# Graph kernel in five sweeps over one adjacency matrix: neighbour masks counted ahead, in the first sweep

## What is computed

```python
# layer 0
Ax = adj @ h;  x += 1 - 0.1*h - 0.01*sum(h*Ax, axis=1)
# layer 1, two hops
for k in range(2): h = tanh(concat([adj @ h, h], axis=1) @ W[k])
# layer 2: only the last 100 neighbours of a row, halved for each later one
support = h @ weight
mask = (adj != 0); rank = cumsum(mask, axis=1); deg = rank[:, -1:]
k = minimum(deg, 100); pos = rank - (deg - k)
w = mask * where(pos > 0, 0.5 ** (k - pos), 0)
x += w @ support + bias
# layer 3
h1 = tanh(concat([h, t], axis=1) @ W1 + b1)
x += h1 @ W2 + b2 + adj @ (h @ B.T) - sum(adj, axis=1) * (h @ B.T)
```

## Time and profile before

| | us |
|---|---|
| median of 3 runs | 831.64 (830.78 to 833.84) |
| the profiled execution | 832.51 |
| its span, first to last instruction | 830.7 |
| PE busy | 739.1 (89%) |
| DVE busy | 445.3 (54%) |
| ACT busy | 200.5 (24%) |
| POOL busy | 126.3 (15%) |
| DMA, over the whole span | 275.16 MB, 331 GB/s |

### The profile page before, as it was taken

How to read it: one execution, slowest core, us unless ns; L and a number is a source line. 1 busy time by engine, 2 the same in 40 slices (tenths; PEclk the granted TensorE clock), 3 DMA queues, 4 the chain that set the end, 5 groups by cost and what they waited for, 6 DMA issues and landing times.

```text
span 830.7 us, 10008 instructions
## 1 busy us (share of the span) xinstructions
PE 739.1 (89%) x3717; PEld 293.7 (35%) x3736; DVE 445.3 (54%) x765; ACT 200.5 (24%) x287; POOL 126.3 (15%) x148
## 2 busy tenths in 40 slices
PE   3877878889999999999999798889888979999998
PEld 1222222223433344444444243334333433343333
DVE  5111111147666676767667788888888852111110
ACT  2000000000100000100001576566656640211111
POOL 5001111110000001221112201101110113322221
PEclk9999999999999999999999899999999999999999
DMA  9999999999999999999899666667666747999995
GB/s 375 416 420 419 421 420 421 419 375 376 398 389 389 388 385 346 342 359 334 336 361 362 223 226 221 241 222 266 216 246 221 266 165 277 349 348 368 374 360 208
DMA packets 45984, 275.16 MB, mean 331 GB/s; under 512 B 5104, under 2 KB 13424, under 8 KB 13552
## 3 DMA queue, kind: packets, MB, share of 16 engines
q1 hardware_dynamic: 36720, 266.13, 83.0%
q10 hardware_dynamic: 9216, 8.39, 3.0%
HBM read 270.31 MB, written 4.19 MB: 330 GB/s over the span
## 4 chain that ended last, share of the span: by engine, by line
PE 44%; DMA 27%; DVE 22%; issue 4%; POOL 2%; ACT 1%; DVEq 1%; POOLq 0%
PE accA L922 31%; DMA land<-adj_blocks 26%; DVE uS L757 16%; PE tr L822 2%; PE spare L934 2%; PE spare L937 2%; PE nat L846 1%; PE nat L842 1%; PE accA L947 1%; POOL rstd L434 1%; PE spare L877 1%; DVE uS L740 1%; DVE st L626 1%; PE nat L838 1%; DMA xin<-x_rows 1%
## 5 line engine op out<-in xcount | busy, mean ns | idle before, releaser
L922 PE MATMUL accA<-land,X 128*64 128x512 f32 x1504 | 352.5, 598 | 23.1 <-DMA land<-adj_blocks 21.9
L922 PEld LDWEIGHTS accA<-land,X 128*64 128x64 f32 x1504 | 100.7, 136 | 214.4 <-issue 144.5
L582 ACT ACTIVATE wS<-spare 128x1024 uint16<-128x1024 f32 x128 | 131.0, 1024 | 86.7 <-PE spare L937 84.1
L922 PE MATMUL accA<-cache,X 128*64 128x512 f32 x544 | 131.9, 605 | 22.1 <-DVE X L787 12.6
L757 DVE SCALAR_TENSOR_TENSOR uS<-land,uS 128x512 bf16<-128x512 f32 x180 | 128.5, 714 | 19.7 <-DVE uS L757 0.5
L934 PE MATMUL spare<-uS,triA 128*128 128x512 bf16 x248 | 94.7, 386 | 31.2 <-DVE uS L757 28.4
L441 POOL TENSOR_TENSOR hS<-tS 128x256 f32<-128x256 f32 x32 | 25.7, 805 | 561.8 <-DVE tS L627 561.8
L937 PE MATMUL spare<-uS,triB 128*128 128x512 bf16 x246 | 94.3, 383 | 0.5 <-ACT wS L582 0.2
L740 DVE TENSOR_TENSOR wS<-wS,land 128x512 f32<-128x512 f32 x96 | 66.8, 695 | 39.4 <-DMA land<-adj_blocks 36.8
L740 DVE TENSOR_TENSOR uS<-uS,land 128x512 f32<-128x512 f32 x92 | 64.6, 702 | 32.4 <-DMA land<-adj_blocks 29.6
L947 PE MATMUL accA<-wS,X 128*128 128x512 bf16 x247 | 74.5, 381 | 0.3
(11 more groups left out here) (76 smaller groups left out, 436.2 us busy)
## 6 DMA issues: line engine op xcount, KB each, us to landing
land<-adj_blocks SPq DMA_DIRECT2D x235, 1024.0 KB, 7.6
cache<-adj_blocks SPq DMA_DIRECT2D x17, 1024.0 KB, 12.8
xin<-x_rows ACTq DMA_DIRECT2D x32, 128.0 KB, 6.2
x_rows<-zS ACTq DMA_DIRECT2D x24, 128.0 KB, 4.7
cache<-x_rows SPq DMA_DIRECT2D x1, 1024.0 KB, 4.9
out_rows<-zS ACTq DMA_DIRECT2D x8, 128.0 KB, 7.0
wts<-weights SPq DMA_DIRECT2D x1, 675.0 KB, 6.2
cache<-triangles SPq DMA_DIRECT2D x1, 128.0 KB, 6.0
```

The costliest lines, as they stand in the source:

```text
L582: nc.scalar.activation(weights(c, b).bitcast(U16), spare[:, 2 * k:2 * k + 2, :].rearrange("p a b -> p (a b)"), ACT.Relu)\
L922: last = nc.tensor.matmul(accA[k * D:(k + 1) * D, c % 2, :], tile(X[p % 2], TQ * b + k), of[:, k * W:(k + 1) * W], start=(b == 0), stop=(b ...
```

## The change

- L0 now also makes the masks: DVE writes the mask of a whole block (two tiles, 1024 elements, bfloat16) in one instruction, and PE multiplies it with a 0/1/128 matrix (`count`), one block behind the sweep, into `spare`. For each tile this gives, per row of the matrix, the count of non-zero entries in all later tiles. After each chunk ACT copies one half of the result, DVE adds the other, and an ACT DMA writes it to DRAM (`counts_d`).
- L2 passes the matrix forward. DVE makes plain masks, one instruction for a block, of 127 partitions; the 128th partition is filled by small DMAs from the counts (`counts_for`, one for each pair, on SP's queue). So one triangular matrix for a tile does, with the count of later tiles as one of its terms: the second matmul of each tile goes.
- Partition 127 of each tile is then missing from the weights. It is done apart for each chunk: SP loads these 32 rows (`left_over`, nine small DMAs), POOL makes their weights in three instructions, and PE adds them in one matmul. The features of that partition take a way through DRAM once (`left_d`, `loS`).
- Two of the 16 evictions of weights of a chunk (blocks 4 and 12) go from ACT to DVE, three blocks late in DVE's list.
- Row sums: 10 blocks in L1A, 6 in L1B (before 8 and 8).
- 16 pairs are cached, 48 are loaded in each later sweep. The eight mask places are of a whole block. A place in `land` is free in L0 only after the masks too.

```diff
 def cached_pairs(c):
-    return (0, 1, 4) if c == 0 else (0, 4)
+    return (0, 4)
...
+TOTALS = {L1A: (1, 2, 4, 5, 7, 9, 10, 12, 13, 15), L1B: (0, 3, 6, 8, 11, 14)}
...
+MASKS = 8
+AHEAD = 3
+EVAC_DVE = (4, 12)
+EVAC_LAG = 3
...
+        def weights_out(eng, ops, c, b):
+            n = NQ * c + b
+            eng.wait_ge(tri_done, n + 1)
+            if n >= WRING:
+                eng.wait_ge(w_used, n - WRING + 1)
+            k = b % 2
+            w, of = weights(n).bitcast(U16), spare[:, 2 * k:2 * k + 2, :].rearrange("p a b -> p (a b)")
+            if b in EVAC_DVE:
+                ops.tensor_scalar(w, of, 0.0, None, ALU.max).then_inc(w_ready_dve, 1)
+            else:
+                ops.activation(w, of, ACT.Relu).then_inc(w_ready, 1)
...
+            def counts_for(g):
+                if g < MASKS // 2:
+                    sp.wait_ge(sums_done, 2 * g + 2)
+                else:
+                    sp.wait_ge(tri_done, 2 * (g - MASKS // 2) + 2)
...
+                sp.dma_start(uS[LAST:P, at:at + 2 * BLK].rearrange("o (t w) -> o t w", w=W),
+                             tile_counts[c, 4 * k:4 * k + 4, 0].rearrange("(o t) w -> o t w", o=1))\
+                    .then_inc(counts_in[g % (MASKS // 2)], 16)
+            def left_over(c):
+                if c:
+                    sp.wait_ge(left_ready, c)
+                rows = adj_in.rearrange("(b p) (t w) -> p b t w", p=P, t=2 * TQ)
+                for k in range(PAIRS):
+                    sp.dma_start(loadjS[4 * k:4 * k + 4, :], rows[LAST, c * PAIRS + k]).then_inc(left_in, 16)
+                sp.dma_start(locntS[:, :], tile_counts[c, :, 1]).then_inc(left_in, 16)
+            def after_masks(g):
+                for i in range(counts_to[0], min(g + AHEAD, PAIRS * NC - 1) + 1):
+                    counts_for(i)
+                    counts_to[0] = i + 1
+                if g % PAIRS == 3 and g // PAIRS + 1 < NC:
+                    left_over(g // PAIRS + 1)
+                if g == 6:
+                    sp.wait_ge(copy_used, copied_no(L1B, NC - 1, 1) + 1)
+                    sp.dma_start(left_d, X[1][LAST:P, :].bitcast(F16)).then_inc(left_rows, 16)
+                    sp.wait_ge(left_rows, 16)
+                    sp.dma_start(loS[:, :], left_d.rearrange("o (t w) -> (o t) w", w=2 * D)).then_inc(left_rows, 16)
...
             def step(p, c, before, before2):
-                for k in pair_order(p):
+                if p == L2 and c == 0:
+                    sp.wait_ge(counts_out, 16 * NC)
+                    left_over(0)
+                    after_masks(0)
+                for k in range(PAIRS):
...
-                        if pp == L2:
-                            sp.wait_ge(u_ready, NT * pc + 2 * (NQ - 1 - 2 * pk) + 2)
-                        else:
+                        if pp != L2:
                             sp.wait_ge(swept, sweep_no(pp, pc, 2 * pk + 1) + 1)
+                        if pp in (L0, L2):
+                            sp.wait_ge(u_ready, mask_no(pp, pc, 2 * pk + 1) + 1)
...
+                    if n >= LAND and pp == L2:
+                        after_masks(PAIRS * pc + pk)
...
+            def left_over(c):
+                w = left_weights(c)
+                pool.wait_ge(left_in, 16 * (PAIRS + 1) * (c + 1))
...
+                nc.gpsimd.tensor_scalar(loadjS[:, :], loadjS[:, :], 0.0, -NEIGH * BIT, ALU.is_equal, ALU.mult)\
+                    .then_inc(left_step, 1)
...
+                nc.gpsimd.tensor_tensor(loadjS[:, :], loadjS[:, :], locntS[:, :], ALU.subtract).then_inc(left_step, 1)
...
+                nc.gpsimd.tensor_scalar(w, loadjS[:, :], NEIGH * BIT, 0.0, ALU.add, ALU.max).then_inc(left_ready, 1)
...
+                if p == L0 and at == 4:
+                    act.wait_ge(counted, NQ * (c + 1))
+                    if c:
+                        act.wait_ge(count_ready, c)
+                    nc.scalar.activation(upperS, spare[D:P, c % 2, :], ACT.Copy).then_inc(count_half, 1)
+                if p == L0 and at == 7:
+                    act.wait_ge(count_ready, c + 1)
+                    act.dma_start(counts_d[c], countS).then_inc(counts_out, 16)
...
                     if at == 7:
                         norm_rows(p, c, chunk(X[1], c))
+                        dve.wait_ge(count_half, c + 1)
+                        if c:
+                            dve.wait_ge(counts_out, 16 * c)
+                        nc.vector.tensor_tensor(countS, upperS, spare[0:D, c % 2, :], ALU.add).then_inc(count_ready, 1)
...
-                            nc.vector.scalar_tensor_tensor(out=u, in0=of, scalar=0.0, in1=earlier,
-                                                           op0=ALU.not_equal, op1=ALU.add).then_inc(u_ready, 1)
+                if p in (L0, L2):
+                    n = NQ * c + b
+                    wait_landed(dve, p, c, b)
+                    if n >= MASKS:
+                        dve.wait_ge(counted if p == L0 else tri_done, n - MASKS + 1)
+                    elif p == L2:
+                        dve.wait_ge(sums_done, b + 1)
+                    rows = P if p == L0 else LAST
+                    nc.vector.tensor_scalar(masks(b)[0:rows, :], block_of(p, c, b)[0:rows, :], 0.0, None, ALU.not_equal)\
+                        .then_inc(u_ready, 1)
+                if p == L2 and b - EVAC_LAG in EVAC_DVE:
+                    weights_out(dve, nc.vector, c, b - EVAC_LAG)
...
+            def count(c, b):
+                pe.wait_ge(u_ready, mask_no(L0, c, b) + 1)
+                if b == 0 and c >= 2:
+                    pe.wait_ge(count_ready, c - 1)
+                for k in range(TQ):
+                    t = TQ * b + k
+                    last = nc.tensor.matmul(spare[k * D:(k + 1) * D, c % 2, :], later[:, 2 * (NT - t):2 * (2 * NT - t)],
+                                            masks(b)[:, k * W:(k + 1) * W], start=(b == 0), stop=(b == NQ - 1))
+                last.then_inc(counted, 1)
...
+            def triangle(c, b):
+                n, g = NQ * c + b, PAIRS * c + b // 2
+                pe.wait_ge(u_ready, mask_no(L2, c, b) + 1)
+                pe.wait_ge(counts_in[g % (MASKS // 2)], 16 * (g // (MASKS // 2) + 1))
+                if n >= 2:
+                    weights_ready(n - 2)
+                for k in range(TQ):
+                    last = nc.tensor.matmul(spare[:, 2 * (b % 2) + k, :], triA[:, :], masks(b)[:, k * W:(k + 1) * W],
+                                            start=True, stop=True)
                 last.then_inc(tri_done, 1)
...
+                if b == NQ - 1:
+                    pe.wait_ge(left_ready, c + 1)
+                    if c == 0:
+                        pe.wait_ge(left_rows, 32)
+                    nc.tensor.matmul(accA[:, c % 2, :], loS[:, :], left_weights(c).bitcast(BF16),
+                                     start=False, stop=True).then_inc(weighed, 1)
```

More of the change, by code:

```diff
@@ L60, in cached_before @@
     return sum(len(cached_pairs(k)) > i for k in range(c))
[L63 to L70, removed]
 LAND = 4
-LOADS = [(p, c, k) for p in range(5) for c in range(NC) for k in pair_order(p) if (c, 2 * k) not in CACHE_SLOT]
+LOADS = [(p, c, k) for p in range(5) for c in range(NC) for k in range(PAIRS) if (c, 2 * k) not in CACHE_SLOT]
 LOAD_NO = {what: i for i, what in enumerate(LOADS)}
@@ L136, in norm_no, with mask_no, evac_no @@
     return PRO_GROUPS + row_no(p, c)
-HELD = 2
+MASKS = 8
+AHEAD = 3
 WRING = 4
[L145 to L166, removed]
+EVAC_DVE = (4, 12)
+EVAC_LAG = 3
+LAST = P - 1
+def mask_no(p, c, b):
+    return (0 if p == L0 else NQ * NC) + NQ * c + b
+def evac_no(c, b):
+    on_dve = sum(k in EVAC_DVE for k in range(NQ))
+    if b in EVAC_DVE:
+        return on_dve * c + EVAC_DVE.index(b)
+    return (NQ - on_dve) * c + sum(k not in EVAC_DVE for k in range(b))
 LATE = (8,)
@@ L476, in step @@
                         split_rows(before[1])
+                if p == L2 and c + 1 < NC:
+                    left_over(c + 1)
                 if p == L3 and c:
@@ L941, in weigh @@
-            def weigh(c, pair):
-                pe.wait_ge(w_ready, NQ * c + pair + 1)
-                first = 2 * weigh_order(c)[0]
-                for i in range(2):
-                    t = 2 * pair + i
-                    w = weights(c, pair)[:, i * W:(i + 1) * W].bitcast(BF16)
-                    last = nc.tensor.matmul(accA[:, c % 2, :], tile16(NT - 1 - t), w,
-                                            start=(t == first), stop=(t == NT - 1))
-                last.then_inc(w_used, 1)
+                if p == L0 and b:
+                    count(c, b - 1)
+                elif p == L0 and c:
+                    count(c - 1, NQ - 1)
@@ new lines, in weigh @@
+            def weigh(c, b):
+                n = NQ * c + b
+                weights_ready(n)
+                if c == 0 and b % 2 == 0:
+                    pe.wait_ge(copy_used, copied_no(L1B, b // 2, 1) + 1)
+                for k in range(TQ):
```

(15 more changed lines are left out.)

121 lines of the change are left out of this document (55 added, 66 removed).

## The result

The changed kernel takes 795.55 us (median of 4 runs, 788.66 to 798.05) against 831.21 for the kernel before: ratio 0.9553, 95% interval 0.9485 to 0.962. The forecast was 773, in a range of 755 to 798: faster, as said, but by 36 us where 58 were forecast. The execution whose profile is shown took 788.66 us, the fastest of the four, its span is 786.6. Runs of this kernel lie 9 us apart, those of the kernel before 3.5; part of that shows in the clock of L2, as experiment 1 tells.

A forecast was written before the change was run, and what follows sets the result against it. The prediction took loads (DMA) to bound L0, PE to bound L1A and L1B, DVE to bound L2. Its terms, +4 + 1 - 4.5 - 15 - 45 = -59.5 us, from 832.5 gave 773, range 755 to 798.

The forecast's parts named there:

- Masks, evictions, counts beside the sweep: Prices: 0.67 us a mask in L0, 1.23 a DVE eviction in L2; L0's counts, 3.4 a chunk on PE, hidden.
- L0's start, "4 us later": In L0, the fifth load waits for masks until 23.2, DMA idles from 21.2 to 25.6, L0 ends 4 us later.
- L1A, "+1": L1A: ten blocks of row sums stay below PE; L0's last count and layer norm add 1 us (0 to 3).
- L1B, "-4.5": L1B: fewer row sums on DVE remove most of PE's gaps, layer norm waits included: 4.5 us less (0 to 6).
- L2's start, "15 less": L2's first two chunks end at t0 + 49 after the sweep's end t0, before t0 + 63.6: 15 us less (11 to 20).
- The stall that was forecast instead: L2, chunk 1: PE's list stands still 6 us at block 1 for `loS`, landing at t0 + 32.5 but needed at t0 + 26.
- L2 steady, "20.0": L2's later chunks: DVE's list takes 20.0 us a chunk; six chunks at 20.0 in place of 27.6, 45 less.
- POOL's lock: In steady L2, masks stand still while POOL works in SBUF: 2.8 us a chunk (0 to 4.9).
- POOL holds up DVE in full: Rival, L2: all 4.9 us of POOL count and layer norms come late, 3.5 a chunk more, 794 us; chance 0.17.
- L0 becomes PE's: Rival, L0: counts don't run side by side, PE needs 21.8 a chunk against 20.6, 10 us more, 783; chance 0.08.

The follow-up runs named there:

- experiment 1: The changed kernel run again, unaltered, against the kernel before: 792.17 us (median of the three executions that count), ratio 0.9504.
- Experiment 2: Changed kernel with PE taking up the counts in chunk 0 of L0 only from block 6 on: 794.65 us, 0.9542 of the kernel before.
- experiment 4: Changed kernel with row sums of eight blocks each in L1A and L1B again: 794.8 us, 0.9546 of the kernel before.
- experiment 11: Changed kernel with late first L0 counts, L2's first loads before the row-sum wait, and early x rows in L2: 780.79 us, 0.9378 of the kernel before.
- experiment 10: Changed kernel with x rows loaded early in L2 and no count transfers there behind the first four pairs: 787.67 us, 0.9461 of the kernel before.
- Experiment 3: Changed kernel with L2's loads of pairs 1, 2, 3 and 5 issued before SP's wait for row sums: 786.75 us, 0.944 of the kernel before.
- experiment 6: Changed kernel with POOL's three instructions for left-over rows on 8 columns in place of 512: 800.63 us, 0.9596 of the kernel before.
- experiment 5: Changed kernel with L2's x rows loaded at block 13 of the chunk before: 789.27 us, 0.946 of the kernel before.
- experiment 7: Changed kernel without L2's count transfers behind the first four pairs, nor the waits for them: 800.24 us, 0.9609 of the kernel before.
- experiment 9: Changed kernel with x rows loaded early in L2 and POOL's three instructions on 8 columns: 784.72 us, 0.944 of the kernel before.

## Why the prediction was right and wrong

- **Masks, evictions, counts beside the sweep**: right. 0.70 and 1.22 were measured for 0.67 and 1.23. L0's chunks behind the first are 20.8 apart against 20.7 before, so the loads still set the pace and PE's 3.4 us of counts hide.
- **L0's start, "4 us later"**: the step failed in what it left out. It looked at when DVE has the masks, and not at PE's list, where the first count waits for the first mask with the sweep of blocks 2 and 3 behind it. Experiment 2 takes that away and gets the issue time of the forecast, and 2 of the 8 us. The idle time of DMA, 4.4 in the forecast, was met at 4.6 although the load left 2 us late, which is luck: with the load on time it was 2.5. And a second term was put at nothing: bytes. The prediction called the 64 KB of counts a chunk hidden because ACT has time; where the loads set the pace they cost DMA's time, 1.1 us for the 0.5 MB, a part of the 3.2 us of transfers that came on top.
- **L1A, "+1"**: +3.5 in the first profile, +1.3 to +5.8 over the others. Chunk 1 takes part of it through the sums (experiment 4). PE's waits for loads, 1.3 us in L1A before the change, are 3.6 in the first profile and 5.8 in experiment 11, which has the longest L1A; why the loads come later stays open.
- **L1B, "-4.5"**: -3.4 in the first profile, but between 0 and -3.7 over all with this code. The term was taken from PE's wait for the layer norm, which went from 5.4 to 1.1 in the first profile, while 1.3 of waits for loads came up. In experiment 10, where L1B takes 147.3, that wait is 4.2: to have most of it gone was too much.
- **L2's start, "15 less"**: 7.1 less. Two steps failed. The row sums of DVE, put behind the third mask, were not followed: a load that comes late delays them, and they delay PE's first triangle, ACT's copy, and the mask that frees a place. Nor was the low clock's length foreseen: 2 us were put down for it, and PE worked for 12 at half speed. The stall that was forecast instead, six microseconds for the rows that go through DRAM, didn't come: that round trip took 3.7 us (issue at 490.66, the next at 494.33), not 10. Experiment 3 supports the reading: with four loads issued earlier PE's first triangle comes 3.1 us behind the sweep's end, not 9.1, and chunk 0 is 7 us shorter. It doesn't part the order in DVE's list from the lateness of the loads as such.
- **L2 steady, "20.0"**: 20.1, met in part by luck. The list has DVE busy 19.1 of a chunk, with 0.9 of waits on top; it is busy 16.2. Masks start 0.60 apart where 0.70 was put down (the six in 3.69 at the start of L0), which is 1.6 of the difference, and POOL's lock is 2.1 (from the masks' 0.81 and 0.86 against 0.69) where 2.8 was put down. Waits fill the chunk up: in the last seven 7.1 us for POOL, as listed, but also 10.0 for PE's triangles ahead of the two evictions and 4.9 for xin. Moreover a forecast in which DVE's list is the bound says that relieving DVE helps, and experiment 6 shows that by itself it doesn't. What stands beside it is a wait that wasn't in the sum: the x rows of the epilogue, needed 5.4 us after their issue in experiment 1 where it had been 10.8 before the change (issued at 544.11, used at 554.92), and landing after 5.8, at most 8.2, where it had been 3.1, now that DMA is busy in L2. How much of the 20.1 hangs on it the runs leave open: with xin early L2's last seven chunks were no shorter (experiment 5), while the reliefs of experiments 6 and 7 were 12 to 13 us slower without it (experiments 9 and 10).
- **Rivals**: "POOL holds up DVE in full", 794, comes closest to the 795.6 measured, and is yet not what happened. The lock is real and was in the sum. The missing time lies elsewhere: of the 15.7 us between the forecast and the profiled execution 11.6 are the two starts and 2.5 L1A, and the 7 more up to the median are not in that profile; experiment 1 suggests chunks of L2 with a sagging clock. *L0 becomes PE's* is settled by the counts: four take 0.60 (the row of 22.79 in experiment 2), as long as two matmuls of L2 one behind the other (0.59), so they do run side by side. The Trainium skill ("SBUF — State Buffer", "SBUF: two separate sides") says that the loser blocks for the whole instruction. The longest mask agrees: it took 1.63 against 0.69, began at 575.35 inside an instruction of POOL of 1.47 (from 574.96) and ended 0.55 behind it. But the full price of the first rival was not this kernel's: the lock came to 2.1 a chunk where 4.9 would be all of it.

## What to carry to other kernels

When a stage gets faster, list every transfer whose issue and use lie a fixed number of blocks apart: the distance shrinks with the stage (here from 10.8 to 5.4 us) while the landing time can grow (here from 3.1 to between 5.5 and 8.3, with one or two 1 MB loads issued just ahead), and such a transfer can cancel a further relief. When a wait is added to an engine's list, follow what stands behind it on that engine, the row sums here and the sweep there, before anything else. An eviction moved from one engine to another relieves the first but ties two lists together; try it without.

## What the runs showed of the hardware

POOL's two one-input instructions with two operations on 32 partitions of 512 took 2.29 and 2.46 us, beside 1.27 for its two-input one of the same size, where 1.22 had been put down for all three from a two-input row of 128 partitions. Fewer partitions did not make the two-input one quicker. These means have waits for DVE in them. At the start of L2, with DVE idle, the three took less:

```profile
461.00 1.94 POOL L536 TENSOR_SCALAR loadjS<-loadjS 32x512 f32<-32x512 f32 x1
463.02 1.14 POOL L539 TENSOR_TENSOR loadjS<-loadjS,locntS 32x512 f32<-32x512 f32 x1
464.25 1.92 POOL L541 TENSOR_SCALAR lowS<-loadjS 32x512 uint16<-32x512 f32 x1
```

PE's clock fell behind short pauses in steady L2: in experiment 1 matmuls at half the pace follow pauses of 2.6, 2.3, 2.1 and 1.7 us, while in the first profile pauses of up to 2.1 us went by with the clock at 1.00. The length of the last pause alone doesn't decide.
